# A decoder layer on one core: constant products for TensorE, squares added on VectorE, and new orders on all engines

## The reference, cut to what matters

```
# part 1: linear attention with decay, 16 heads of 16, chunks of 128
h = layernorm(x);  q, k, v = h @ Wq, h @ Wk, h @ Wv;  q, k = rotary(q), rotary(k)
inter  = (q * q_decay) @ kv            # kv: the state of the chunks before
intra  = ((q @ k.T) * dmask) @ v       # dmask: decay by distance, per head
kv_new = r_C * kv + (k * k_decay).T @ v
attn   = inter + intra
x = x + (attn * rsqrt(mean(attn**2) + 1e-5) * rms_w) @ Wo
# part 2: probabilities over 256 context rows are added to x
kv  = ctx @ W_k.T + b_k
sim = (layernorm(x) @ kv) @ kv.T / 16
x = x + softmax(norm(sim) * gamma + beta)
# part 3: 8 experts, the best 2 for each token
h = layernorm(x);  gate = softmax over the two best of h @ Wr, zero elsewhere
for e in range(8):  x = x + gate[:, e] * (h @ We[e] + be[e])
```

## Time and profile before

| | us |
|---|---|
| median of three runs | 149.0 |
| the runs | 149.0, 150.75, 147.78 |
| time of the profiled execution | 148.25 |
| its span, from the first to the last instruction | 145.9 |
| TensorE busy | 130.7 (90%) |
| VectorE busy | 101.3 (69%) |
| ScalarE busy | 72.8 (50%) |
| GpSimd busy | 31.6 (22%) |
| mean granted TensorE clock | 0.96 |

### The profile page before, as it was taken

How to read it: one execution, slowest core, us unless ns; L and a number is a source line. 1 busy time by engine, 2 the same in 40 slices (tenths; PEclk the granted TensorE clock), 3 DMA queues, 4 the chain that set the end, 5 groups by cost and what they waited for, 6 DMA issues and landing times.

```text
span 145.9 us, 3109 instructions
## 1 busy us (share of the span) xinstructions
PE 130.7 (90%) x1063; PEld 98.0 (67%) x1063; DVE 101.3 (69%) x330; ACT 72.8 (50%) x228; POOL 31.6 (22%) x58
## 2 busy tenths in 40 slices
PE   0799989999866999999998999999999997699990
PEld 0455677886544797876777887767787676487870
DVE  0454899459797761764998659799846849879553
ACT  4278648979897015578437639440143453411300
POOL 7125400630820200102262040103002113020110
PEclk9999999999997558999999999999999999999998
DMA  3999980000000000000000002000002000002002
GB/s 117 286 363 315 351 228 2 7 0 4 0 0 0 4 0 4 0 0 0 0 2 7 0 4 72 0 0 2 4 0 74 4 0 0 0 6 66 0 0 72
DMA packets 7934, 7.29 MB, mean 50 GB/s; under 512 B 2264, under 2 KB 7792, under 8 KB 7792
## 3 DMA queue, kind: packets, MB, share of 16 engines
q1 hardware_dynamic: 7424, 6.79, 14.7%
q10 hardware_dynamic: 496, 0.32, 0.8%
HBM read 6.06 MB, written 1.05 MB: 49 GB/s over the span
## 4 chain that ended last, share of the span: by engine, by line
PE 58%; DVE 11%; SPq 9%; ACT 6%; issue 6%; DMA 4%; POOL 3%; DVEq 1%; ACTq 0%; POOLq 0%
PE ebank L1104 25%; PE chain L1234 5%; DMA xin<-in_x 4%; PE chain L1104 4%; PE front L1104 4%; PE chain L1259 4%; PE chain L1219 3%; PE front L1309 2%; DVE acc L977 2%; PE front L1096 2%; DVE zg L893 2%; SPq L314 2%; DVE probs L861 2%; PE chain L1248 2%; DVE zb L897 1%
## 5 line engine op out<-in xcount | busy, mean ns | idle before, releaser
L1104 PE MATMUL ebank<-w_e_hi,h3T_hi 128*128 128x512 f32 x56 | 20.0, 438 | 2.3 <-DVE acc L977 1.5
L861 DVE TENSOR_TENSOR probs<-chain,dec 128x512 f32<-128x512 f32 x32 | 19.9, 679 | 0.0
L977 DVE SCALAR_TENSOR_TENSOR acc<-ebank,gate_y,acc 128x256 f32<-128x256 f32 x40 | 17.4, 476 | 3.4 <-PE ebank L1104 3.2
L1104 PE MATMUL ebank<-w_e_hi,h3T_lo 128*128 128x512 f32 x56 | 18.0, 403 | 0.0
L1104 PE MATMUL ebank<-w_e_lo,h3T_hi 128*128 128x512 f32 x56 | 18.0, 403 | 0.0
L1104 PEld LDWEIGHTS ebank<-w_e_hi,h3T_hi 128*128 128x128 f32 x56 | 9.2, 193 | 6.1 <-DVE acc L977 3.1
L1104 PEld LDWEIGHTS ebank<-w_e_lo,h3T_hi 128*128 128x128 f32 x56 | 10.8, 193 | 2.6
L1104 PEld LDWEIGHTS ebank<-w_e_hi,h3T_lo 128*128 128x128 f32 x56 | 10.8, 193 | 2.6
L1219 PE MATMUL chain<-qx,kT 32*128 32x256 f32 x128 | 9.4, 405 | 2.3 <-DVE probs L861 1.8
L358 POOL TENSOR_TENSOR rot_b<-qk,cst 128x128 f32<-128x128 f32 x16 | 7.6, 495 | 17.2 <-ACT qk L492 17.2
L1234 PE MATMUL chain<-probs,vpad 128*32 128x128 f32 x256 | 9.5, 311 | 0.5 <-issue 0.5
(11 more groups left out here) (180 smaller groups left out, 294.4 us busy)
## 6 DMA issues: line engine op xcount, KB each, us to landing
w_e<-in_L_ffn_We SPq DMA_DIRECT2D x2, 1024.0 KB, 9.1
xin<-in_x SPq DMA_DIRECT2D x4, 256.0 KB, 5.1
dec<-in_decay SPq DMA_DIRECT2D x1, 1024.0 KB, 6.7
out<-outb SPq DMA_DIRECT2D x8, 128.0 KB, 1.8
w_qkv<-in_L_attn_Wq SPq DMA_DIRECT2D x1, 256.0 KB, 4.2
w_qkv<-in_L_attn_Wk SPq DMA_DIRECT2D x1, 256.0 KB, 4.6
w_qkv<-in_L_attn_Wv SPq DMA_DIRECT2D x1, 256.0 KB, 4.8
w_o<-in_L_attn_Wo SPq DMA_DIRECT2D x1, 256.0 KB, 6.9
```

Of the source, the lines that this page charges most:

```text
L861: nc.vector.tensor_tensor(probs[:, t, r], chain[:, r], dec[:, r], ALU.mult).then_inc(s_sc, 1)
L977: nc.vector.scalar_tensor_tensor(out=outb[:, t, :] if last else acc[:, t, :], in0=expert_bank(b, q, t)[:, (e % 2) * D:(e % 2 + 1) * D], sc ...
L1104: mm = pe.matmul(dst, a[ka][:, c, a_cols], b[kb][:, c, b_cols], start=(n == 0 and c == 0), stop=(n == 2 and c == KC - 1))
```

## The change

- A tile `warm` (it lies in `acc`, which is not used until the first expert is added) is set to 1.0 by VectorE as its first instruction. TensorE no longer begins with the wait for the constants; it multiplies `warm` by itself five times (`keep_clock`), and the wait moves into the steps that read constants. The three `keep_clock` calls of before are gone.
- `keep_warm` is new: the same 256-column product into `ebank1`. It stands six times: once before and three times after `transpose_qk(2,1)`, and behind each of the two `transpose_x2(0,...)`.
- `add_squares` is new on VectorE: it adds the second group of `sqT` to the first, and `square_sums` has one matmul for a tile instead of two.
- The call lists of all engines but SyncE are written in new orders.

```diff
+        warm = acc[:, 0]
...
             x_rstd(0)
+            rotary_cross(0,0)
+            rotary_cross(0,1)
+            keys_for_states(0)
             x_rstd(1)
...
+            rotary_cross(2,0)
             x1_variance(0)
-            rotary_cross(2,0)
+            keys_for_states(2)
             sim_rstd(0)
...
         def _(dve):
+            nc.vector.memset(warm, 1.0).then_inc(s_warm, 1)
...
+            def add_squares(b, t):
+
+                dve.wait_ge(s_at, TILES * b + t + 1)
+                nc.vector.tensor_tensor(sqT[:, t, 0, :], sqT[:, t, 0, :], sqT[:, t, 1, :], ALU.add).then_inc(s_sqt, 1)
...
         def _(pe):
-            pe.wait_ge(s_cst, 16)
-
-            def keep_clock(dst, cols):
-
-                pe.matmul(dst[:, 0:cols], ident, cst[:, 0:cols], start=True, stop=True)
+            pe.wait_ge(s_warm, 1)
+
+            def keep_clock(dst):
+
+                pe.matmul(dst[:, 0:2 * P], warm[:, 0:P], warm, start=True, stop=True)
+
+            def keep_warm():
+
+                pe.wait_ge(s_state, 2)
+                pe.wait_ge(s_qkT, TILES * 2)
+                pe.wait_ge(s_qd, 2)
+                pe.matmul(ebank[1][:, 0:2 * P], warm[:, 0:P], warm, start=True, stop=True)
...
             def square_sums(b):
 
                 for t in range(TILES):
-                    pe.wait_ge(s_at, TILES * b + t + 1)
-                    for g in range(GROUPS):
-                        mm = pe.matmul(ss_ps(t), sqT[:, t, g, :], onescol[:], start=(g == 0), stop=(g == GROUPS - 1))
+                    pe.wait_ge(s_sqt, TILES * b + t + 1)
+                    mm = pe.matmul(ss_ps(t), sqT[:, t, 0, :], onescol[:], start=True, stop=True)
                     mm.then_inc(s_ss, 1)
```

More of the change, by code:

```diff
@@ L986, in _ @@
             rotate(0,0)
+            rotate(0,1)
+            scale_wo()
             low_weights(1)
             low_weights(2)
-            rotate(0,1)
             x_low(1,0)
-            scale_wo()
             x_low(1,1)
@@ L995, in _ @@
             mask_states(0)
+            decay_queries(0)
             x_stats(2)
-            decay_queries(0)
             decay_scores(0,1,0)
             decay_scores(0,1,1)
-            x_stats(3)
             x_low(2,0)
             rotate(1,0)
+            x_stats(3)
+            rotate(1,1)
+            add_squares(0,0)
+            add_squares(0,1)
             rms_variance(0)
@@ L1006, in _ @@
             low_experts(0)
+            decay_queries(1)
+            rotate(2,0)
+            sim_variance(0)
             low_small()
-            rotate(1,1)
-            sim_variance(0)
-            rotate(2,0)
             softmax_input(0)
+            mask_states(1)
             rotate(2,1)
-            residual2(0,0)
             decay_scores(1,0,0)
             decay_scores(1,0,1)
-            decay_queries(1)
+            residual2(0,0)
             decay_queries(2)
-            mask_states(1)
             mask_states(2)
@@ L1025, in _ @@
             route(0)
+            add_squares(1,0)
+            add_squares(1,1)
             rms_variance(1)
-            add_experts(0,0)
             residual1(1)
             x_low(3,0)
+            add_experts(0,0)
             low_experts(1)
+            sim_variance(1)
             x_low(3,1)
-            sim_variance(1)
             softmax_input(1)
@@ L1037, in _ @@
             rotate(3,0)
-            rotate(3,1)
             decay_scores(2,1,0)
             decay_scores(2,1,1)
+            residual2(1,0)
+            add_experts(0,2)
+            rotate(3,1)
+            add_squares(2,0)
+            add_squares(2,1)
+            decay_queries(3)
+            rms_variance(2)
             mask_states(3)
-            decay_queries(3)
-            add_experts(0,2)
-            residual2(1,0)
             residual2(1,1)
+            residual1(2)
             x2_low(1,0)
-            rms_variance(2)
-            residual1(2)
             x2_low(1,1)
@@ L1059, in _ @@
             decay_scores(3,1,1)
+            add_experts(1,2)
             residual2(2,0)
-            add_experts(1,2)
             residual2(2,1)
+            add_squares(3,0)
+            add_squares(3,1)
+            rms_variance(3)
             x2_low(2,0)
+            residual1(3)
+            x2_low(2,1)
             add_experts(1,3)
-            rms_variance(3)
-            x2_low(2,1)
-            residual1(3)
             route(2)
@@ L1368, in _ @@
             project_qk(1,1)
+            transpose_x(2,1)
             attend(0)
@@ L1381, in _ @@
             transpose_context(1)
+            states(1)
             similarities(0)
@@ L1384, in _ @@
             project_qk(2,1)
-            states(1)
-            transpose_qk(1,1)
+            transpose_qk(2,0)
             transpose_keys(1)
             scores(1,0)
-            transpose_qk(2,0)
+            states(2)
+            keep_warm()
             transpose_qk(2,1)
-            states(2)
+            keep_warm()
+            keep_warm()
+            keep_warm()
             scores(1,1)
             transpose_x2(0,0)
+            keep_warm()
             transpose_x2(0,1)
+            keep_warm()
             expert(0,0,0)
@@ L1418, in _ @@
             scores(2,0)
-            project_qk(3,1)
+            project_qk(3,0)
             expert(0,2,0)
@@ L1422, in _ @@
             transpose_qk(3,0)
+            project_qk(3,1)
             expert(0,2,1)
-            transpose_qk(3,1)
             states(3)
             attend(2)
+            transpose_qk(3,1)
             expert(0,3,0)
-            transpose_x2(1,0)
             square_sums(2)
             project(2,0)
+            transpose_x2(1,0)
+            project(2,1)
             transpose_x2(1,1)
-            project(2,1)
+            expert(0,3,1)
             transpose_x1(2,0)
-            expert(0,3,1)
             transpose_x1(2,1)
@@ L1454, in _ @@
             expert(1,3,0)
+            square_sums(3)
             transpose_x2(2,1)
-            expert(1,3,1)
-            square_sums(3)
             project(3,0)
             project(3,1)
+            expert(1,3,1)
             transpose_x1(3,0)
```

148 lines of the change are left out of this document (74 added, 74 removed).

## The result

| | median, us | runs, us |
|---|---|---|
| changed kernel | 141.87 | 141.84, 141.9, 141.91, 141.2 |
| kernel before, same rounds | 149.58 | 149.0, 150.75, 147.78, 150.16 |

The ratio is 0.955, with a 95% interval of 0.947 to 0.963: faster. (Each ratio here compares the undisturbed runs of both kernels; the kernel before has times from 146.8 to 151.95, so a ratio can lie above that of the medians.) The prediction was 144.0 us in 140.8 to 148.0: right in direction and range, 2.1 us too slow. The profiled execution of the changed kernel took 141.84 us, 140.0 of them its span.

A forecast was written before the change was run, and what follows sets the result against it. The prediction took TensorE, busy for 90% of the span, as the bound, partly at half clock. From the profiled 148.25 us, -4.3 + 1.1 - 1.2 = -4.4 gave 143.9, taken as 144.0 us, range 140.8 to 148.0.

The forecast's parts named there:

- The clock, -4.3: Constant products before the first expert unit keep the clock up where it was 0.50 from 45.5 to 55.8 us: -4.3 us.
- the thin stretch: TensorE from 41.06 to 44.75 us, busy 1.57 of 3.69 us before the clock fell; four constant products should fit there free.
- What is late next, +1.1: TensorE would then wait for VectorE before attend(1), the transposed gates and the squares: +1.1 us, bounds 0.4 and 2.5.
- The moved unit: Expert unit of 1.4 us moved from directly behind attend(1) to later, leaving TensorE a 0.5 us wait before the gates.
- Squares, -1.2: Half the square_sums matmuls save TensorE 0.4 us in each of three sequences: -1.2 us, bounds -1.6 and +0.6.
- The start, 0: Five early constant products raise the rate sooner, but the wait for x of sequence 2 takes the gain: 0, bounds ±1.
- pin: VectorE's wait for x of sequence 2, arriving at 21.02 us, in which whatever the start wins earlier is lost.
- New orders elsewhere, 0: Reordered GpSimd and VectorE lists, and the 86 us after the dip: taken as 0, bounds -2 and +1.5 for those 86.

The follow-up runs named there:

- e1: Kernel before, old orders, with only the six constant products before the first expert unit added and decay_queries(1) moved ahead: 146.87 us, ratio 0.980.
- e2: Changed kernel without its six constant products before the first expert unit: 142.72 us, ratio 0.950.
- e12: Changed kernel without any constant products and with the squares added by TensorE, so the new orders alone: 145.94 us, ratio 0.978.
- e3: Changed kernel with the two groups' squares added by TensorE again instead of VectorE: 143.83 us, ratio 0.958.
- e6: Changed kernel with expert unit (0,0,1) back directly behind attend(1), ahead of the transposed gates: 142.00 us, ratio 0.950.
- e4: Kernel before, old orders, with all three edits (six constant products, five at the start, squares added on VectorE): 148.10 us, ratio 0.988.
- e11: Kernel before, old orders, with the eleven constant products and squares still added by TensorE: 145.25 us, ratio 0.983.
- e5: Changed kernel without its five constant products at the very beginning: 142.89 us, ratio 0.955.

## Why the prediction was right

By its own steps, against the two traces of each kernel:

- *The clock, -4.3.* Mechanism right: the products fill the thin stretch, the clock holds, and the pieces of the earlier trace rows came near their prices of the earlier trace rows. As a term by itself it measured 3.5 to 3.6 (e1), so it was 0.7 too large. In the new orders it is worth 1.4 where the clock falls (e2) and nothing where it doesn't (e12 without and e3 with the products both take 113.4 us from `attend(0)` on), since these orders cut the stretch at 0.50 to a third or do without it; the prediction gave them nothing. Two small slips leave the sum as it is: the exact rows give 4.3 and the rounded ones 4.4, not the other way round, and 46.73 is the end of one tile's transposes. Both end at 47.14, so that TensorE was idle for 0.58 us and not 1.0.
- *What is late next, +1.1.* Mis-sized: the wait before the gates is 0.34, that before `attend(1)` 0.26, and the squares cost TensorE none. VectorE was 0.9 us sooner than I had it: its last decayed scores end at 49.25 and not at 50.1. The first four now stand ahead of `residual2(0,0)` and hand `scores(1,1)` its banks 0.6 sooner (below, the kernel before and then the changed one); `scores(1,1)` and the transposes behind it at full clock brought another 0.45, for which I had 0.2. I had named this order and booked it at 0, because I took the transposes of x2 to be bound by VectorE's sum. Those of the first tile are not: they come directly behind `scores(1,1)`. The moved unit, which I took for a cost, saves 0.6 (e6).

```profile
42.12 2.48 DVE L861 TENSOR_TENSOR probs<-chain,dec 128x512 f32<-128x512 f32 x4
```

```profile
41.52 2.48 DVE L865 TENSOR_TENSOR probs<-chain,dec 128x512 f32<-128x512 f32 x4
```

- *Squares, -1.2.* Right in size (1.5, e3). Not said: it depends on VectorE's order; in the old one it costs 2.0 (e4, e11).
- *The start, 0.* For the pair of traces from which the sum was made it held: `attend(0)` at 25.2 and 25.5. As a statement on the kernel it is wrong, since I took the wait of one trace for a pin. It holds only when the clock rises early. In the profiled execution of before it had, which fits its time of 0.75 below the median; the products are worth 1.2 to 1.5 at `attend(0)` (e5), and against the second trace the changed kernel is 1.7 to 2.0 ahead there.
- *New orders elsewhere, 0.* The term that failed. With no fall behind `attend(0)` in either trace, old orders (e11, 114.4) and new (e12, 113.4) differ by 1.0 us. From `attend(3)` on, VectorE did not become the bound: 39.7 us against 40.5.

From `attend(0)` on, one edit after the other leads from 118.1 (before) to 114.6 (the six products, e1), 114.4 (the start, e11), 113.4 (the orders, without the products, e12), 113.4 (the products again, e3) and 111.9 (squares): 6.2 us, where the prediction's sum had 4.4. It had the clock 0.7 too large, the squares 0.3 too small, 1.1 us of waits (0.6 are in the trace, and the steps above contain them) and nothing for orders that brought 1.0; these errors partly cancel. The medians moved by 7.7 us. The 1.5 beyond the 6.2 are left to the start. That is a remainder and not a measurement: the start differs by -0.3 to +2.0 us between the traces of the two kernels. The spans make it likely: of the 31 executions of the kernel before with a clock of 0.960 to 0.965, 24 span 147.9 to 148.8 us, as its second trace with the late start, and seven 145.7 to 146.4, as its first. The measured 141.87 lies at the low end of the forecast's own 141.6 to 145.9, the end with no new waits and a start of -1, and that is about what came.

## What to carry to other kernels

Where the bound engine waits in short gaps and the granted clock falls behind them, fill the gaps with work that nobody reads; but look also for the engine that makes it wait, and move what isn't urgent out of its list. Before you call a part of the program pinned by a transfer, take a second trace: a pin that has less than a microsecond of wait in it moves with the start of the same execution. An edit that passes work to another engine is worth what that engine's order makes of it: the same one gave 1.5 us and cost 2.0.

## What the runs showed of the hardware

- The clock fell to 0.50 behind a stretch whose longest idle time was 1.28 us, in both traces of before (1.29 in the second), and stayed there for 10.2 us with TensorE busy for 9.6 to 9.7 of them. Half clock was not left as soon as TensorE was busy: `scores`, transposes, an expert unit and the logits passed at 0.50.
- A thin stretch doesn't always bring the fall. Behind one with an idle time of 1.83 us the clock fell in e2's trace and stayed up in e12's, and by the mean granted clocks five of these two versions' ten executions had a fall somewhere.
- At the start the granted clock reads 1.00 in the profile although a 256-column product takes 1.22 us instead of 0.70; the first rise shows only in durations.
- After five products from 1.17 us on, the traced execution of e11 ran at 0.50 from 8.5 to 15.3 us, TensorE being busy for 6.70 of these 6.80 us, and that of e4 from 9.0 to 12.3 us; eight of these two versions' ten executions have a mean granted clock of 0.988 or less. So such products mostly bring the rise forward (in e3 they did not) but do not keep the clock by themselves; in the old orders there are gaps of 0.45 and 1.18 us for a context transfer and copies just before.
